# Eight linear-attention blocks: one activation table set for exponential and logarithm, and the relu of one Q chunk moved from VectorE to ScalarE

## The reference

```python
q = x @ Wq + bq;  k = x @ Wk + bk;  v = x @ Wv + bv
Q = elu(q) + 1.0
K = elu(k) + 1.0
KV   = sum over tokens of K * v          # one number per feature
Ksum = sum over tokens of K
Z = 1.0 / (Q * Ksum + 1e-6)
V = Q * KV * Z
x = layernorm(gelu(V @ Wo + bo) + x)
x = layernorm(gelu(gelu(x @ Wf1 + bf1) @ Wf2 + bf2) + x)
```

## Time and profile before

| | us |
|---|---|
| median of 3 runs | 1981.09 (1980.33 to 1982.42) |
| profiled execution | 1980.78 |
| its span | 1979.1 |
| PE busy | 1727.0 (87%) |
| DVE busy | 1360.2 (69%) |
| ACT busy | 1143.8 (58%) |
| POOL busy | 285.5 (14%) |

### The profile page before, as it was taken

The page is one execution under the profiler, slowest core; times in us unless marked ns, Lnnn a source line. Parts: engine busy times, 40 slices in busy tenths (PEclk is TensorE's granted clock), DMA queues, the critical chain, the costliest instruction groups (busy, mean ns, idle before and its releaser), DMA issues.

```text
span 1979.1 us, 28184 instructions
## 1 busy us (share of the span) xinstructions
PE 1727.0 (87%) x10420; PEld 766.7 (39%) x10420; DVE 1360.2 (69%) x2664; ACT 1143.8 (58%) x2091; POOL 285.5 (14%) x364
## 2 busy tenths in 40 slices
PE   5798048699999999999979978889888998799999
PEld 4788046122222222222334434444444444444443
DVE  6998876999999999999634365665565656522222
ACT  5465003189989989989853355666566655222222
POOL 3456002300000000000000011111111111111111
PEclk8999569589999999999989999999999999799999
DMA  1000000022100000000103410000000000222331
GB/s 51 1 1 1 0 0 6 36 45 29 15 2 2 2 2 2 2 2 2 33 12 66 89 27 0 17 17 16 1 17 17 17 0 1 43 34 48 49 55 30
DMA packets 72527, 39.12 MB, mean 20 GB/s; under 512 B 22112, under 2 KB 68704, under 8 KB 72400
## 3 DMA queue, kind: packets, MB, share of 16 engines
q1 hardware_dynamic: 71824, 36.65, 9.8%
q10 hardware_dynamic: 576, 0.79, 0.1%
HBM read 34.08 MB, written 3.15 MB: 19 GB/s over the span
## 4 chain that ended last, share of the span: by engine, by line
PE 56%; DVE 30%; ACT 6%; issue 4%; DMA 3%; SPq 1%; POOL 1%; DVEq 0%; ACTq 0%; POOLq 0%
DVE MX L1144 17%; PE PS L1711 6%; PE PS L1717 6%; PE PS L1226 6%; PE PS L2228 4%; PE PS L2229 4%; PE PS L2238 4%; PE PS L1252 4%; PE PS L1662 3%; PE PS L539 3%; PE PS L1681 2%; PE PS L1103 2%; DMA SB<-scr_w 2%; DVE MS L643 2%; PE PS L1488 2%
## 5 line engine op out<-in xcount | busy, mean ns | idle before, releaser
L1285 ACT ACTIVATE tmpb<-PS 128x512 f32<-128x512 f32 x1024 | 554.1, 595 | 76.5 <-PE PS L1252 57.3
L1144 DVE TENSOR_REDUCE MX<-PS 128x2 f32<-128x1024 f32 x512 | 584.5, 1215 | 18.1 <-PE PS L1103 16.1
L1226 PE MATMUL PS<-tmpb,VS 128*32 128x256 f32 x4096 | 328.2, 392 | 1.5 <-ACT tmpb L1285 0.6
L1103 PE MATMUL PS<-KST,QST 56*128 56x512 bf16 x1024 | 205.4, 399 | 18.7 <-DVE MX L1144 17.0
L1252 PE MATMUL PS<-QST,KST 59*128 59x512 bf16 x1024 | 200.8, 389 | 3.5 <-ACT tmpb L1285 0.6
L2263 DVE TENSOR_TENSOR HG<-HG,PS 128x512 f32<-128x512 f32 (+1 forms) x96 | 65.9, 686 | 183.1 <-PE PS L2229 183.1
L2253 ACT ACTIVATE HG<-PS 128x512 f32<-128x512 f32 (+1 forms) x96 | 57.2, 595 | 186.6 <-PE PS L2228 186.6
L1226 PEld LDWEIGHTS PS<-tmpb,VS 128*32 128x32 f32 x4096 | 80.8, 108 | 196.4 <-issue 108.5
L1252 PEld LDWEIGHTS PS<-QST,KST 59*128 59x128 bf16 x1024 | 49.5, 93 | 222.5 <-ACT tmpb L1285 209.3
L1711 PE MATMUL PS<-X,WF 128*128 128x512 f32 x256 | 129.2, 640 | 3.3 <-ACT X L1907 3.1
L1923 ACT ACTIVATE HF<-PS,CL 128x512 f32<-128x512 f32 x128 | 87.9, 687 | 69.5 <-PE PS L1711 69.5
(11 more groups left out here) (337 smaller groups left out, 2533.8 us busy)
## 6 DMA issues: line engine op xcount, KB each, us to landing
SB<-scr_w SPq DMA_DIRECT2D x14, 1024.0 KB, 14.2
WF<-in_L_attn_Wf SPq DMA_DIRECT2D x16, 256.0 KB, 3.0
QST<-NMP SPq DMA_DIRECT2D x192, 1.0 KB
G<-in_L_ffn_w SPq DMA_DIRECT2D x16, 176.0 KB, 2.4
W<-in_L_ffn_w SPq DMA_DIRECT2D x16, 128.0 KB, 2.2
QST<-scr_q SPq DMA_DIRECT2D x14, 128.0 KB
scr_q<-tmpb SPq DMA_DIRECT2D x3, 512.0 KB, 3.6
KST<-scr_k SPq DMA_DIRECT2D x14, 96.0 KB
```

Of the source, the lines that this page charges most:

```text
L1103: pe.matmul(PS[:, b + x, :], QST[r, 2 * g + jj, CH * qc + P * t:CH * qc + P * t + P], KST[r, g, cs(kc)], start=True, stop=True).then_inc(s ...
L1144: r = v.tensor_reduce(MX[:, :, m // (TPC * NC), m // NC % TPC, m % NC], PS[:, b:b + 2, :], AX.X, ALU.max)
L1226: last = pe.matmul(PS[32 * j:32 * j + 32, 3, h], VS[:, kt, u // NC, :], PB[:, kt % 2, j, h], start=(kt == 0 and half == 0), stop=(kt == NT ...
L1285: a.activation(PB[:, kt % 2, j, :], PS[:, at % 3, :], ACT.Exp, scale=HD ** -0.5).then_inc(s_exp, 1)
```

## The change

In each of the eight blocks the table set loaded first becomes one with exponential and logarithm, the load ahead of the logarithms is removed, the relu of Q chunk 3 is taken out of VectorE's program and put behind that chunk's exponential on ScalarE, and the signal to `s_qe` goes with the relu. `act_qr` writes the same tile, ZR, from the same PSUM bank as line 1992 did.

```diff
--- before.py
+++ after.py
@@ -1857,7 +1857,7 @@
         def act_inputs(a, chain, b):
 
             n = NC * b
-            a.preload_act_table_set("exp_and_others")
+            a.preload_act_table_set("natural_log_exp_and_others")
             if b == 0:
                 act_feat4(a, 0)
                 act_qr(a, b, 0)
@@ -1877,8 +1877,8 @@
                 act_feat4(a, 3)
             act_k(a, b, 2)
             act_qr(a, b, 2).then_inc(s_qe, 1)
-            act_qe(a, b, 3).then_inc(s_qe, 1)
-            a.preload_act_table_set("natural_log")
+            act_qe(a, b, 3)
+            act_qr(a, b, 3).then_inc(s_qe, 1)
             a.wait_ge(s_ks, b + 1)
             for h in range(2):
                 a.wait_ge(s_p, n + 2 * h + 2)
@@ -1988,8 +1988,6 @@
             v_k(v, chain, b, 2)
             v.tensor_reduce(KS[:, 1:2], acc[:, 1, :], AX.X, ALU.add).then_inc(s_ks, 1)
             v_p(v, chain, b, 2)
-            v.wait_ge(s_qe, n + NC)
-            chain.link(v.tensor_scalar(ZR[:, 3, :], PS[:, QBANK[3], :], col(b, BQ), 0.0, ALU.add, ALU.max))
             v_p(v, chain, b, 3)
             v.wait_ge(s_ks, b + 1)
             chain.link(v.tensor_scalar(KR[:, :], KS[:, 1:2], 1e-30, None, ALU.max))
```

## The result

The changed kernel takes 1974.39 us (median of 11 runs, 1964.78 to 1975.93) against 1981.5 (1979.62 to 1982.94) for the kernel before, run on the same chip: 7.1 us faster, ratio 0.996 with a 95% interval of 0.995 to 0.997. In a second comparison it took 1971.6 (6 runs, 1965.59 to 1975.42) against 1982.64, ratio 0.994 (0.992 to 0.996). The executions of the changed kernel lie 11 us apart, which its median hides; most of what follows is about that. The profiled execution took 1969.74 us (span 1968.0).

What follows compares the result with a forecast made beforehand. Bound: the joint between layer-1 blocks, where VectorE's pass over the last Q chunk is late, in a TensorE-heavy kernel. 5.9 us (joint) + 5.2 (clock) = 11.1 off 1980.8 gives 1969.7, forecast as 1970.0, range 1966 to 1977.

Steps and rivals of the forecast that it cites:

- Steps 1 to 3: At the block joint: load's removal alone 0.0; VectorE's relu gone, last pair 0.78 us earlier; ScalarE's relu covered by 0.18 us.
- Step 4: Output matmul at the joint: starts 0.52 to 0.78 us earlier, taken as 0.74 a block, 5.9 us over eight blocks.
- Rival B: TensorE's queue keeps the joint's gain at 0.52 or less, clock gives 2 us back: 1975 to 1977; chance 0.12.
- Step 5: TensorE's clock in the stall after the joint: falls cost 8.3 us now, shorter blocks leave 3.1, 5.2 back.
- The sign "one to three" falls: TensorE's clock in layer 1 of the changed kernel: one to three falls expected, not five.
- rival A: TensorE's clock in layer 1 gives nothing back, only the joint's 5.9 us is gained: 1975.2; chance 0.20.
- Rival C: A table load is put back ahead of the first logarithm: 0.3 us later a block, 1983.5; chance 0.05.
- Rival D: A bad stall place against the clock's beat also stays, every block pays 2.9 us: 1990; chance 0.06 with milder forms.

Runs made afterwards that it cites:

- the filled kernels: Two matmul calls, result read by nobody, put into TensorE's 2.75 us stall: kernel before 1971.05 and 1971.71 us, changed kernel 1966.27 and 1965.66.

## Why the prediction was right, and where it was not

Steps 1 to 3 (load, VectorE's relu, ScalarE's relu) held as worked out. The load alone is worth nothing that can be measured (ratio 1.0008, 0.9995 to 1.0022), the relu alone costs 0.32 us a block (0.3 was given), together they gain; the cover of the added wait was 0.17 us (0.18), ScalarE's idle time before the second logarithm 0.22 (0.25).

Step 4 (what is late next) had the bounds 0.52 and 0.78 and took 0.74; the measured value is 0.79, the upper bound within the reading, since the one-column pair overlaps the last warming matmul altogether. Eight blocks give 6.3 us; the filled kernels show 4.8 and 6.05, the first with 1.9 us against it from ahead of layer 1. Rival B is out.

Step 5 (the clock) was about right in what it costs now: 8.3 us by the trace, 9.2 and 9.5 by filling the stall, though a second trace of the kernel before lost only 6.5. It was wrong in what the shorter block does to it. The sentence that failed is "once the stall is at a safe place it should stay there". I had a movement of 0.1 us a block against the beat and took it for nothing; it is 0.04, and over eight blocks even that is not nothing. The sentence that "a fall adds 1.6 and turns it safe again" failed with it: bad places lie up to 2.8 us apart, more than a fall adds, so that falls come in a row. The sign "one to three" falls was missed in two of the three traces. One trace is at a place that stays safe from block 2 to the end (2.6 us lost), the two others slip out of theirs after one and after four safe blocks, and then pay four blocks in a row. So 5.2 us back was the size of a good execution; that the traced one, 1969.74, is what the sum gave for it (1969.7) is luck. In the median of the same runs the clock gave back about 7.1 - 6.3 = 0.8 us, in the second comparison 11.0 - 6.3 = 4.7. The median of 1974.39 is therefore closer to rival A (1975.2) than to the forecast of 1970.0, and the second comparison's gain of 11.0 is at the forecast's 11.1. What spoke for A held, that the beginning's place differs from run to run; what spoke against it held too, since the alternation did break.

The Trainium skill ("TensorE: Matmul & The Clock Gate", "What's actually happening") warns against fitting to a specific count of slow matmuls, as the window runs free of the kernel. The three traces of one kernel agree: 2, 4 and 6 blocks with a fall. For a forecast the term should have been a spread from nothing back to nearly all, not one value; the stated range, 1966 to 1977, had that spread and holds the median.

Rival C did not happen: the loads at lines 1860 and 1888 are eight each, with none between. Rival D's long stretches in block after block came in the kernel with the relu alone, for four blocks. In this kernel a milder form came, four blocks in a row with a fall in two of three traces, and the time stayed below that of the kernel before.

What stays open: that a fall costs 1.0 in one block and 2.0 in another of the same length was read from the traces but not derived; the cause of the scatter ahead of layer 1 (1171.4 to 1173.4) and at its entry is not known; and what makes the beat itself no run here shows.

## What to carry to other kernels

Where two engines hand work to each other at a joint, take the timeline and ask of each edit what is late after it: two edits, of 10.3 and 6.0 us of busy time, gained together 6.3 us at the joint; alone the first gained nothing and the second lost 2.6 there, 7.4 in all. Where TensorE's clock falls in a short stall that comes once per block, a change of block length can move the cost of the clock by as much as the change itself (2.6 us at the joint and 4.6 of the clock with the relu alone); read the distances between block starts, compare several traces, or fill the stall in both kernels before comparing them. Filling alone gained about as much as the change: 9.2 and 9.5 us, against 7.1 and 11.0. The filled changed kernel, at 1966.27 and 1965.66, beats the kernel before by 14.0 and 15.5 us (ratios 0.993 and 0.992, the second with 0.990 to 0.994). It was not run beside the changed kernel; their medians, from different comparisons, are 1974.39 and 1971.6 for that one.

## What the runs showed of the hardware

The wider table set loads in the same 1283 ns as the narrower one; exponential and relu of 512 columns take 0.69 to 0.71 us in both, and the logarithm of 1024 columns 1252 ns against 1242. A switch of sets between an exponential and a logarithm cost more than the load: the two start 2.01 us apart with it and 0.57 without it, so 1.44. Matmuls of one column and their two weight loads hide behind a full matmul: 0.15 us from the pair's start to the next start, where the same pair after an idle time took 0.42. A fall of the clock in an otherwise equal block cost 0.6 to 2.1 us in the changed kernel and 2.3 or 2.4 in three blocks running where the relu alone was moved. Four matmul instructions in a stall, whose result nobody reads, cost nothing in the block (62.28 us with and without them), and none of the 32 blocks of the four filled traces has a fall; the two traces of the kernel before have five and four in eight blocks.
